# Projection moved into the last attention head of a transformer block with routed experts

## The chip, the cores and the metric

The kernel runs on one core of a Trainium2 chip. The metric is device microseconds of one execution, from a launch to its end. Time before: 2275.77 us, the median of 3 runs (2271.68 to 2276.74).

## What is computed

One block of a vision transformer on 48 x 48 tokens (S = 2304) of width C = 384, batch 1, in float32. Attention has 12 heads of 32 columns with a relative position bias by row and by column; then a projection with bias and the residual; then a layer norm, a router that picks 2 of 8 experts for each token, and the experts (384 to 1536, GELU, back to 384), added to the residual.

```
x  = x + proj(softmax(q*scale @ k.T + bias_h + bias_w) @ v) + proj_b     # q, k, v from layernorm(x)
t  = layernorm(x)
x  = x + sum over the 2 best experts of gate * (gelu(t @ W1 + b1) @ W2 + b2)
```

## The kernel before, in words

Every product of precision is made of three: a value is split into a high part (a type that TensorE takes at full rate) and a low part, the rest; high x high, high x low and low x high are added up in PSUM.

The program is a row of stages, each with its own instruction lists for the five engines, and a stage starts when the one ahead has ended on all of them: `phase_qkv`, `phase_rel` (the bias tables), `phase_attention`, `phase_proj`, `phase_gates`, `phase_experts`.

**Attention** (`phase_attention`, L524) goes through the heads 0 to 11, with two sets of buffers for keys, queries and values, by the head's parity `par`. A head has 54 **units**: 3 query blocks of 768 columns (`QB`), with 18 key tiles each. In unit k TensorE makes the scores of unit k + 3 (four matmuls, `scores`, L753) and the product of unit k's weights with the values (four matmuls, `pv`, L769, accumulated over the 18 tiles of a block in `ps_o`, with a row of ones in the values that gives the sums of the softmax), and, for the softmax, two matmuls for the next head's row maxima (`half`, L747, into the two banks of `ps_m`). ScalarE takes the exponential of a unit twice (L849 and L855: `p_hi` and `p_f`); the low part `p_lo` = `p_f` - `p_hi` is made by VectorE for two units of three and by GpSimd for the third (`low`, L604, run at L608). VectorE takes the maxima (L896). From unit 12 (`SHIFT`) of the last head on there is no next head, so no maxima. At the end of a block, in unit 17, 35 or 53, ScalarE and VectorE copy `ps_o` to `o_t` (L866, L913).

SP's list for a head (`rest`, L665) is written out by hand: the next head's keys and values (`load_kv`), then for each block b a wait for its last scores, the next head's query rows (`load_rest`, L633, four transfers, 2.1 MB), the wait for the block's copies and its `store` (L657: values to `o_d`, sums to `sums_d`), and `load_max` (L648: a row of maxima to memory and back); after the third block `load_hi` (L620) for the head after the next, which is needed at unit 12. GpSimd's `joined` (L716) waits for a store and adds the second half of the values to `o_d` by an accumulating transfer. All of SP's transfers are on one queue.

**Projection** (`phase_proj`, L1033): the sums of all heads come back as 216 columns on 128 partitions, VectorE takes the reciprocal (L1189), it goes out to `rec_d` and comes back as 12 rows; TensorE spreads these rows over 128 partitions (L1124), VectorE scales the heads' values by them (`o_f`, L1168) and makes the low part `o_lo` (L1170), ScalarE the high part (L1162), TensorE multiplies by the weights (nine matmuls for each of 18 tiles, L1136), VectorE adds the residual (L1177) and takes the statistics (L1184) for the layer norm. Meanwhile GpSimd adds the bias to x (L1114) and splits the first expert's six weight pieces (`split_piece`, L1020).

**Gates and experts**: `phase_gates` (L1205) normalises, stores the normalised rows (L1326), computes the router and the lists, and loads four pieces of the second expert; `phase_experts` (L1610) gathers rows by expert (L1660) and runs 43 slots of 128 rows; VectorE splits the pieces of the experts 1 to 7 there.

## Time and profile before

| | us |
|---|---|
| median of 3 runs | 2275.77 |
| the profiled execution | 2276.39 |
| its span, first to last instruction | 2274.7 |
| TensorE busy in it | 2056.3 (90%) |
| VectorE, ScalarE, GpSimd busy | 1435.9, 1483.6, 923.9 |
| last copy of the accumulator in the attention | at 1450.41 |
| first instruction of the gates | at 1529.06 |
| first matmul of the experts | at 1631.07 |

Times in the rows are microseconds from the span's start, and durations follow them; a duration marked ns, or behind "busy us, mean", is in nanoseconds. PE is TensorE, PEld its weight loads, DVE VectorE, ACT ScalarE, POOL GpSimd, SPq SP's queue of transfers. What stands in brackets behind a row is the time for which the engine idled ahead of it, and what ended that.

### The profile page before, as it was taken

The numbers are of one execution on the slowest core, as the hardware profiler recorded it, in microseconds if no ns is written. First come the engines' busy times: TensorE is split into PE (matmuls) and PEld (weight loads), VectorE is DVE, ScalarE is ACT, GpSimd is POOL, SyncE is SP. The second block draws the span as 40 slices with busy tenths as digits, with TensorE's granted clock in tenths as the row PEclk, the third lists the DMA queues.
The fourth block names the chain that finished last, engine by engine and source line by source line (L and its number), as shares of the span: only waits on it lengthen the run. The fifth ranks groups of instructions, "written<-read, shape, count | busy, mean of one in ns | idle before, by whom it ended". The sixth has DMA issues, their size and how long they took to land. (4 is left out here: it accounts for less than half of the span.)

```text
span 2274.7 us, 34244 instructions
## 1 busy us (share of the span) xinstructions
PE 2056.3 (90%) x11132; PEld 1798.3 (79%) x11132; DVE 1435.9 (63%) x2321; ACT 1483.6 (65%) x2533; POOL 923.9 (41%) x621
## 2 busy tenths in 40 slices
PE   6955589999999999999999999674799999999998
PEld 6932278888888888888888888462688888989997
DVE  5665669999999999999999996386333443120000
ACT  3354078888888888888888889412255555555554
POOL 0061323333333333333333334380555665565553
PEclk9955789999999999999999999787699999999999
DMA  6698934565446555564565544322433443211111
GB/s 211 219 252 273 179 82 75 115 109 107 94 87 132 88 112 92 108 126 78 106 113 106 101 78 100 107 110 86 160 80 107 142 123 101 46 40 29 29 29 15
DMA packets 92823, 247.02 MB, mean 109 GB/s; under 512 B 10169, under 2 KB 44441, under 8 KB 88421
## 3 DMA queue, kind: packets, MB, share of 16 engines
q1 hardware_dynamic: 81024, 223.57, 41.2%
q0 software_dynamic: 10672, 20.46, 5.4%
q8 instruction: 101, 1.65, 0.3%
q10 hardware_dynamic: 960, 0.80, 0.1%
q14 instruction: 66, 0.53, 0.1%
HBM read 179.27 MB, written 65.52 MB: 108 GB/s over the span
## 5 line engine op out<-in xcount | busy, mean ns | idle before, releaser
L896 DVE TENSOR_REDUCE mx<-ps_m 128x1 f32<-128x384 f32 x1212 | 642.4, 553 | 100.5 <-PE ps_m L751 95.2
L608 POOL TENSOR_TENSOR p_lo<-p_f,p_hi 128x768 fp32r<-128x768 f32 x216 | 403.1, 1866 | 715.5 <-ACT p_f L855 715.5
L849 ACT ACTIVATE p_hi<-ps_s 128x768 fp32r<-128x768 f32 x648 | 529.1, 817 | 135.5 <-PE ps_s L765 132.1
L855 ACT ACTIVATE p_f<-ps_s 128x768 f32<-128x768 f32 x648 | 525.8, 811 | 13.2 <-POOL p_lo L608 13.2
L751 PE MATMUL ps_m<-key_hi,query_hi 128*128 128x384 f32 x1240 | 419.7, 345 | 43.5 <-DMA query_hi<-rel_hi_d 30.9
L608 DVE TENSOR_TENSOR p_lo<-p_f,p_hi 128x768 fp32r<-128x768 f32 x432 | 427.5, 990 | 39.5 <-ACT p_f L855 38.5
L762 PE MATMUL ps_s<-query_hi,key_hi 128*128 128x384 f32 x1296 | 338.1, 342 | 12.5 <-DMA query_rest<-m_d 10.4
L775 PE MATMUL ps_o<-p_hi,val 128*65 128x384 f32 x1296 | 331.4, 337 | 5.2 <-POOL p_lo L608 5.0
L765 PE MATMUL ps_s<-query_rest,key_rest 121*128 121x384 f32 x1296 | 331.8, 337 | 0.0
L775 PE MATMUL ps_o<-p_lo,val 128*65 128x384 f32 x1296 | 331.2, 337 | 0.0
L751 PEld LDWEIGHTS ps_m<-key_hi,query_hi 128*128 128x128 f32 x1240 | 232.2, 189 | 89.2 <-DMA query_hi<-rel_hi_d 31.2
L1670 POOL TENSOR_TENSOR h_lo<-h_f,h_hi 128x512 fp32r<-128x512 f32 x129 | 185.7, 1440 | 258.4 <-ACT h_hi L1798 256.1
L1782 ACT COPY z_sb<-ps_z 128x512 f32<-128x512 f32 x129 | 75.8, 588 | 265.4 <-PE ps_z L1724 265.4
L762 PEld LDWEIGHTS ps_s<-query_hi,key_hi 128*128 128x128 f32 x1296 | 231.4, 189 | 21.9 <-issue 11.4
L765 PEld LDWEIGHTS ps_s<-query_rest,key_rest 121*128 121x128 f32 x1296 | 238.0, 189 | 0.0
L1724 PE MATMUL ps_z<-w_ring,xg_hi 128*128 x774 | 223.8, 397 | 4.8 <-POOL xg_lo L1666 4.8
L1745 PE MATMUL ps_o<-w_ring,h_hi 128*128 x1032 | 214.7, 350 | 11.6 <-POOL h_lo L1670 11.6
L775 PEld LDWEIGHTS ps_o<-p_lo,val 128*65 128x65 f32 x1296 | 175.2, 135 | 50.6
L775 PEld LDWEIGHTS ps_o<-p_hi,val 128*65 128x65 f32 x1296 | 175.9, 136 | 33.4 <-POOL p_lo L608 8.5
L1745 PEld LDWEIGHTS ps_o<-w_ring,h_hi 128*128 128x128 f32 x1032 | 175.4, 188 | 15.4 <-issue 15.2
L1724 PEld LDWEIGHTS ps_z<-w_ring,xg_hi 128*128 128x128 f32 x774 | 144.6, 189 | 29.0 <-issue 5.2
L1792 ACT ACTIVATE h_f<-ps_h,b_sb 128x128 f32<-128x128 f32 x516 | 147.8, 370 | 6.7 <-issue 1.2
(247 smaller groups left out, 2242.7 us busy)
## 6 DMA issues: line engine op xcount, KB each, us to landing
query_rest<-rel_lo_d SPq DMA_DIRECT2D x36, 864.0 KB
query_rest<-qk_lo_d SPq DMA_DIRECT2D x36, 576.0 KB
query_rest<-qk_hi_d SPq DMA_DIRECT2D x36, 576.0 KB
query_hi<-rel_hi_d SPq DMA_DIRECT2D x12, 864.0 KB, 17.0
w_raw__19867<-w_u SPq DMA_DIRECT2D x12, 768.0 KB, 5.3
w_raw__19868<-w_u SPq DMA_DIRECT2D x12, 768.0 KB, 4.6
w_raw__19869<-w_u SPq DMA_DIRECT2D x12, 768.0 KB, 4.4
w_raw__19870<-w_u SPq DMA_DIRECT2D x12, 768.0 KB, 4.4
```

The lines of the kernel that those rows point to most:

```text
L608: engine.tensor_tensor(p_lo[r][:], p_f[idx % 2], p_hi[r][:].bitcast(F32), ALU.subtract).then_inc(lo_done(0, idx)[0], 1)
L751: pe.matmul(ps[:, c, 0:TB], query_hi[tp][:, tile], key_hi[tp][:, keys], start=True, stop=True).then_inc(mm_ok, 1)
L762: pe.matmul(ps_s[:, bank + c, 0:TB], key_hi[par][:, j * P:(j + 1) * P], query_hi[par][:, b * QB + c * TB:b * QB + (c + 1) * TB], start=Tru ...
L765: last = pe.matmul(ps_s[:, bank + c, 0:TB], key_rest[par][:, j * P:(j + 1) * P], query_rest[b][:, j // 3, c * TB:(c + 1) * TB], start=Fals ...
L775: last = pe.matmul(ps_o[0:VW, c, 0:TB], val[par][:, j, :], part[r][:, c, :], start=(j == 0 and part is p_hi), stop=(j == TILES - 1 and par ...
L849: act.activation(p_hi[r][:], ps_s[:, bank:bank + 2, 0:TB], ACT.Exp).then_inc(hi_ok, 1)
L855: act.activation(p_f[idx % 2], ps_s[:, bank:bank + 2, 0:TB], ACT.Exp).then_inc(f_ok, 1)
L896: dve.tensor_reduce(mx[s // TILES][:, s // 3 % 6, col:col + 1], ps_m[:, c, 0:TB], AX.X, ALU.max).then_inc(mx_ok, 1)
L1670: pool.tensor_tensor(h_lo[u % H_RING][:], h_f[u % 2][:], h_hi[u % H_RING][:].bitcast(F32), ALU.subtract).then_inc(hlo_ok, 1)
L1724: last = pe.matmul(ps_z[:, u % 2, :], v[s % 2][:, k, :], moe.ring[:, cols], start=(n == 0), stop=(n == 8))
L1745: last = pe.matmul(ps_o[:, s % 2, 0:C], v[u % H_RING][:, b, :], moe.ring[:, cols], start=(c == 0 and n == 0), stop=(c == CHUNKS - 1 and n ...
L1792: last = act.activation(h_f[u % 2][:, b, :], ps_h[:, u % 2, b, :], ACT.Gelu, bias=bias)
```

## The change

`phase_proj` is taken out. Heads are numbered from 0; the last is head 11.

- **SP** (`rest`): `store` moves ahead of the wait for the block's scores and of `load_rest`, in every head. In head 10, behind the query loads of its first block, the sums of heads 0 to 7 are loaded (`flat_early`), and their values into `room`; after its second block the reciprocals go out to `rec_d`. After its third block come eight `spread` transfers (each a row of `rec_d` broadcast to 32 partitions of `share`), the sums and values of heads 8 to 10, x, their reciprocals and three more `spread` rows, and `load_max` of the last head's third block behind all of these. The projection's weights are loaded at the end of head 8's list.
- **GpSimd**: `joined` of the last head's blocks goes. In head 10 it makes the high parts of the projection's weights, in the last head the high parts (`high_part`) of the 18 tiles.
- **VectorE**: in head 10 at unit 22 it waits for `flat_early` and takes the reciprocal. In the last head: low parts of the weights (`low_weights`, units 1 and 2); nine products `scale` of `room` by `share` (units 4, 5, 6, 8, 9, 10 and 18, 19, 20), a second reciprocal at unit 12; then, by tile, `low_part` two units ahead of the product and `added` one unit behind it.
- **TensorE** (`tail`): 18 tiles ("all") of nine matmuls over heads 0 to 10 and the bias, in units 26 to 48, and 18 tiles ("own") of three matmuls over head 11 straight from its accumulator copy, with two columns more that give its sums: six in units 29 to 34, six in units 43 to 48, and six after the last unit. They take turns with the two banks of `ps_m`.
- **ScalarE** copies both halves of `ps_o` as high parts in the last head, VectorE subtracts for the low parts; `added` divides an own tile by its sums (a reciprocal of one column, then a multiply-add).
- **Weight pieces**: the first four are loaded at the start of the gates in place of the second expert's first four; GpSimd splits two of them there, and SP waits for each split before it loads the fifth and sixth piece, ahead of the third and fourth store of the normalised rows. VectorE splits the other four at the start of the experts.
- Buffers are placed so that x, `share` and the parity-0 keys and queries can share room.

```diff
+EARLY = 2 * HPT
+LATE = HEADS - 1 - EARLY
+FIRST_TILE = 26
+SPLITS_AT = [11, 14]
+WEIGHTS_AT = [1, 2]
+SCALES_AT = [4, 5, 6, 8, 9, 10, 18, 19, 20]
+SPLIT_EARLY = 2
...
+            steps.setdefault(FIRST_TILE + 4 * t // 3, []).append(("all", t))
+            steps.setdefault((29 + t if t < TPQ else 37 + t) if t < 2 * TPQ else UNITS, []).append(("own", t))
...
+            def load_x(g):
+
+                rows = slice(g * TPQ, (g + 1) * TPQ)
+                sp.wait_ge(scaled, QBLOCKS * (g + 1))
+                sp.dma_start(x1[:, rows, :], x.rearrange("(t p) c -> p t c", p=P)[:, rows, :]).then_inc(x_in[g], 16)
+
+            def joins(n):
+                for g in range(2):
+                    sp.wait_ge(ot_out[g], 16 * ((n + 1 - g) // 2))
+                    sp.wait_ge(low_out[g], 16 * ((n + 1 - g) // 2))
+
+            def spread(c, heads):
+                for h in range(heads):
+                    row = rec_d[c * HPT + h:c * HPT + h + 1, :].broadcast_to([HD, S])
+                    sp.dma_start(share[h * HD:(h + 1) * HD, c, :], row).then_inc(spread_in[c], 16)
+
             def rest(h, par):
                 sp.wait_ge(pv_ok, UNITS * h + RING)
                 load_kv(h + 1, 1 - par)
                 for b in range(QBLOCKS):
 
+                    store(h, par, b)
                     sp.wait_ge(s_ok, UNITS * h + TILES * (b + 1))
                     load_rest(h + 1, b)
-                    store(h, par, b)
+                    if h == HEADS - 2 and b == 0:
+                        joins(QBLOCKS * EARLY)
+                        sp.dma_start(flat_early[:], flat(sums_d, 0, EARLY)).then_inc(sums_in, 16)
+                        for c in range(2):
+                            sp.dma_start(room[:, c, :], o_d[c * P:(c + 1) * P, :]).then_inc(early_in, 16)
+                    if h == HEADS - 2 and b == 1:
+                        sp.wait_ge(rec_ok, 1)
+                        sp.dma_start(flat(rec_d, 0, EARLY), flat_early[:]).then_inc(rec_out, 16)
                     if b < 2:
                         load_max(h + 1, b)
                 if h < HEADS - 2:
                     sp.wait_ge(s_ok, UNITS * (h + 1) + LEAD)
                     load_hi(h + 2, par)
+                else:
+                    sp.wait_ge(s_ok, UNITS * (h + 1))
+                    sp.wait_ge(rec_out, 16)
+                    for c in range(2):
+                        spread(c, HPT)
+                    joins(QBLOCKS * (HEADS - 1))
+                    sp.dma_start(flat_late[:], flat(sums_d, EARLY, LATE)).then_inc(sums_in, 16)
+                    sp.wait_ge(raw_zero, 5)
+                    sp.dma_start(room[0:P - HD, 2, :], o_d[2 * P:C - HD, :]).then_inc(late_in, 16)
+                    load_x(0)
+                    sp.wait_ge(rec_ok, 2)
+                    sp.dma_start(flat(rec_d, EARLY, LATE), flat_late[:]).then_inc(rec_out, 16)
+                    sp.wait_ge(rec_out, 32)
+                    spread(2, LATE)
                 load_max(h + 1, 2)
+                if h == HEADS - 4:
+                    load_weights()
+                if h == HEADS - 2:
+                    load_x(1)
+                    load_x(2)
...
+            def tail(kind, t):
+
+                n = number_of[kind, t]
+                if n == 0:
+                    pe.wait_ge(mx_ok, 2 * UNITS * HEADS)
+                if n >= 2:
+                    pe.wait_ge(evicted, n - 1)
+                if n == 0:
+                    pe.wait_ge(w_low, 2)
+                if kind == "all":
+                    pe.wait_ge(low_ok, t + 1)
+                    hi, lo = part_hi[t % len(part_hi)], lows[:, :, t * P:(t + 1) * P]
+                    for m, (v, w) in enumerate([(hi, w_hi), (hi, w_lo), (lo, w_hi)]):
+                        for k in range(KC):
+                            last = pe.matmul(ps_m[:, n % 2, 0:C], v[:, k, :], w[:, k, :], start=(m + k == 0), stop=(m == 2 and k == KC - 1))
...
+            def scale(n):
+
+                c, cols = n // QBLOCKS, slice(n % QBLOCKS * QB, (n % QBLOCKS + 1) * QB)
+                rows = P if c < 2 else P - HD
+                if n == 0:
+                    dve.wait_ge(early_in, 32)
+                if n == 6:
+                    dve.wait_ge(late_in, 16)
+                if n % QBLOCKS == 0:
+                    dve.wait_ge(spread_in[c], 16 * (HPT if c < 2 else LATE))
+                dve.tensor_tensor(room[0:rows, c, cols], room[0:rows, c, cols], share[0:rows, c, cols], ALU.mult).then_inc(scaled, 1)
...
+                    if h == HEADS - 2 and k == TILES + 4:
+                        dve.wait_ge(sums_in, 16)
+                        dve.reciprocal(flat_early[:], flat_early[:]).then_inc(rec_ok, 1)
+                    if last and k in WEIGHTS_AT:
+                        low_weights(WEIGHTS_AT.index(k))
+                    if last and k in SCALES_AT:
+                        scale(SCALES_AT.index(k))
+                    if last and k == 12:
+                        dve.wait_ge(sums_in, 32)
+                        dve.reciprocal(flat_late[:], flat_late[:]).then_inc(rec_ok, 1)
...
+                    if last:
+                        for job in order:
+                            if unit_of[job] == k + 2 and job[0] == "all":
+                                low_part(job[1])
+                        for job in order:
+                            if unit_of[job] == k - 1:
+                                added(*job)
...
-            for i in range(PIECES, PIECES + RAWS):
+            for i in range(RAWS):
                 moe.load_piece(sp, i)
+            sp.dma_start(moe.b1_sb[:], moe.b1_t).then_inc(moe.b_in, 16)
             for blk in range(BLOCKS):
+                if 2 <= blk < 2 + SPLIT_EARLY:
+                    sp.wait_ge(moe.w_ok, blk - 1)
+                    moe.load_piece(sp, RAWS + blk - 2)
                 sp.wait_ge(xn_ok, blk + 1)
...
+            for part in range(SPLIT_EARLY, PIECES):
+                moe.split_piece(dve, part)
             for e in range(1, EXPERTS):
```

## Rows read from the trace of the kernel before

**Rows 1.** By stage: window, us, busy PE, PEld, DVE, ACT, POOL, clock, DMA, GB/s

```profile
1270.00:1367.00 97.00, 96.04 (x543) 85.35 (x543) 87.94 (x151) 83.40 (x114) 35.71 (x21) 1.00 0.54 102
1398.00:1424.00 26.00, 25.60 (x145) 21.21 (x143) 13.96 (x13) 25.77 (x37) 11.81 (x7) 1.00 0.38 122
1450.40:1529.00 78.60, 51.78 (x198) 40.99 (x198) 48.22 (x51) 8.58 (x8) 53.62 (x22) 0.76 0.39 130
1479.00:1529.00 50.00, 43.40 (x186) 37.35 (x186) 40.27 (x46) 5.80 (x5) 44.97 (x16) 0.88 0.22 83
```

**Rows 2.** Timeline, start and duration in us: the end of the attention and the gates' beginning

```profile
1450.41 0.48 ACT L866 COPY o_t<-ps_o 65x384 f32<-65x384 f32 x1 [2.89 <-PE ps_o L775]
...
1529.06 0.29 SPq L1321 DMA_DIRECT2D b_raw<-b  x1
```

**Rows 3.** Timeline of VectorE in the projection: three additions of the residual

```profile
1509.98 1.47 DVE L1177 TENSOR_TENSOR x<-ps_y,x 128x384 f32<-128x384 f32 x3
```

**Rows 4.** Timeline of TensorE in the projection: two groups of three matmuls

```profile
1490.40 0.68 PE L1136 MATMUL ps_y<-pw_lo,o_hi 128*128 128x384 f32 x3
1490.92 0.68 PE L1136 MATMUL ps_y<-pw_hi,o_lo 128*128 128x384 f32 x3
```

**Rows 5.** Timeline of GpSimd in head 10: the join of the first block

```profile
1320.97 0.78 POOL L721 DMA_DIRECT2D o_d<-o_t  x1 [4.40 <-DMA o_d<-o_t]
```

**Rows 6.** Timeline of ScalarE: the accumulator's copies at units 17, 35, 53 of head 10

```profile
1302.12 0.48 ACT L866 COPY o_t<-ps_o 65x384 f32<-65x384 f32 x1 [0.23 <-PE ps_o L775]
...
1335.10 0.48 ACT L866 COPY o_t<-ps_o 65x384 f32<-65x384 f32 x1 [0.23 <-PE ps_o L775]
...
1367.22 0.48 ACT L866 COPY o_t<-ps_o 65x384 f32<-65x384 f32 x1 [0.23 <-PE ps_o L775]
```

**Rows 7.** Timeline of SP's queue: `load_hi`; stores of head 10; query loads

```profile
1272.38 0.42 SPq L625 DMA_DIRECT2D query_hi<-rel_hi_d  x1
...
1303.04 1.25 SPq L661 DMA_DIRECT2D o_d<-o_t  x1
...
1364.81 0.43 SPq L642 DMA_DIRECT2D query_rest<-qk_lo_d  x1
...
1368.07 0.32 SPq L661 DMA_DIRECT2D o_d<-o_t  x1
```

**Rows 8.** Transfers' size and us to landing: issued at 1272.38, 1303.04, 1368.07

```profile
query_hi<-rel_hi_d SPq DMA_DIRECT2D x1, 864.0 KB, 18.1
...
o_d<-o_t SPq DMA_DIRECT2D x1, 96.0 KB, 17.6
...
o_d<-o_t SPq DMA_DIRECT2D x1, 96.0 KB, 13.2
```

**Rows 9.** Timeline of TensorE: the first maximum of unit 12 of head 10

```profile
1293.04 0.34 PE L751 MATMUL ps_m<-key_hi,query_hi 128*128 128x384 f32 x1
```

**Rows 10.** Timeline of VectorE: units 22 (head 10), 4 (last head); the projection's preparations

```profile
1311.55 0.56 DVE L896 TENSOR_REDUCE mx<-ps_m 128x1 f32<-128x384 f32 x1 [0.31 <-PE ps_m L751]
...
1376.65 0.56 DVE L896 TENSOR_REDUCE mx<-ps_m 128x1 f32<-128x384 f32 x1 [0.34 <-PE ps_m L751]
...
1460.56 1.50 DVE L1189 RECIPROCAL rflat<-rflat 128x216 f32<-128x216 f32 x1 [9.59 <-DMA rflat<-sums_d]
...
1466.70 1.36 DVE L1191 TENSOR_TENSOR pw_lo<-pw_raw,pw_hi 128x1152 fp32r<-128x1152 f32 x1 [4.64 <-ACT pw_hi L1157]
```

**Rows 11.** As rows 1, in the projection: a gap of TensorE and after it

```profile
1516.20:1520.10 3.90, 0.51 (x3) 0.19 (x2) 3.90 (x3) 0.00 (x0) 3.90 (x2) 1.00 0.00 0
...
1521.30:1524.20 2.90, 2.90 (x11) 2.90 (x11) 1.72 (x4) 0.00 (x0) 2.90 (x1) 0.50 0.00 0
```

**Rows 12.** What the transfers moved from 1364 to 1384, in 40 slices

```profile
GB/s 0 0 0 86 98 276 276 221 221 215 221 215 215 203 197 227 258 147 141 152 160 178 154 141 141 141 119 98 68 43 49 37 12 0 0 0 0 43 98 55
```

**Rows 13.** Timeline of GpSimd in the projection: a piece's subtraction

```profile
1503.95 3.49 POOL L1030 TENSOR_TENSOR w_ring<-w_raw__19869,w_ring 128x1536 fp32r<-128x1536 f32 x1
```

**Rows 14.** Groups from 1483.9 to 1501.7: busy us, mean ns | idle before

```profile
L1170 DVE TENSOR_TENSOR o_lo<-o_f,o_hi 128x1152 fp32r<-128x1152 f32 x3 | 10.1, 3354 | 3.7 <-ACT o_hi L1162 3.7
```

365 lines of the change are left out of this document (174 added, 191 removed).

## The prediction

> **What bounds the kernel now.** I read the busy time by stage first, then the seams between stages on the timeline, then SP's queue with its transfers' landings. In the attention TensorE is busy 96.0 of the 97.0 us of a head; VectorE, at 87.9, is close behind it, so work added to VectorE there is not free [rows 1]. From unit 12 of the last head on the maxima are over: VectorE is busy 14.0 of 26 us, while TensorE (25.6) and ScalarE (25.8) share the bound. In the 78.6 us that follow TensorE is busy only 51.8, at a mean clock of 0.76: transfers, reciprocals and VectorE set the pace of the projection, and that is the stretch which the change removes. Gates and experts keep their order but for the weight pieces.
>
> The sum is made against the profiled execution, 2276.39 us (span 2274.7 and 1.7 around it), which is 0.6 above the median of 2275.77. A measurement of this kernel can tell a change of about 0.2%, 4.6 us.
>
> **1. The stage that goes.** ScalarE's last copy of the accumulator starts at 1450.41 and the first instruction of the gates at 1529.06 [rows 2]: 78.65 us. In its place stands what follows the last product with the values: two copies of 0.48 and the subtractions behind them, so that the first own product starts some 1.2 us later, and then six own tiles, which VectorE paces: a multiply-add from PSUM (0.5, a third of the 1.47 of three additions [rows 3]), a statistics call of the same length, a reciprocal of one column, and waits between the three. That is 1.0 us for a tile at least; I take 1.3, so 7.8 for six, and 0.5 for the last statistics, 0.3 for the change of stage, 1 for latencies: 10.8. **-67.8 us** (-70 to -65).
>
> **2. The products move into the last head.** A tile's nine matmuls cost three times 0.52, as groups of three start 0.52 apart at full clock [rows 4]: 1.57. Eighteen of these and twelve own tiles of three matmuls (0.52) are 34.5 us of TensorE, in units 26 to 48. Little of it hides, since TensorE and ScalarE were both full [rows 1]: I take off 1.2 for what slack there was, and add 2.1 for tiles that wait for VectorE. **+35.4** (32 to 43).
>
> **3. The store goes ahead of the next head's loads.** Now GpSimd's `joined` waits for a store that lies behind 2.1 MB of query loads, 4.40 us at 1320.97 [rows 5]; its next p_lo is then late, ScalarE waits for it and TensorE for ScalarE. The block in which that falls takes 32.98 us (copies at 1302.12 and 1335.10), the next 32.12 [rows 6]. Over heads 1 to 10 the ten blocks of this kind take 10.3 us more than 32.06 each. With the store ahead of the loads the wait has no cause. **-10** (-13 to -6).
>
> **4. The price of that order.** In the third block the query loads began 3.3 us ahead of the store (1364.81 and 1368.07 [rows 7]); now they begin 0.6 behind it, 3.9 later. Behind them lies `load_hi`, whose last part is issued at 1272.38 and lands 18.1 later, at 1290.5 [rows 7, 8]; the first maximum that needs it runs at 1293.04 [rows 9]. So 2.5 of slack against 3.9: up to 1.4 late here, by the same reckoning less in most other heads. **+3.5** over ten heads (0 to 12).
>
> **5. A new wait in head 10.** `flat_early` is issued behind the query loads of the first block, and VectorE waits for it at unit 22. What stands behind these loads now, the store issued at 1303.04, lands 17.6 us later, at 1320.6 [rows 7, 8]; unit 22's first maximum runs at 1311.55 [rows 10]. So VectorE stands for 9.1 us and then takes the reciprocal of 144 columns (1.50 x 144/216 = 1.0 [rows 10]). TensorE stops one unit later, as each half of `ps_m` waits for its maximum, and so do p_lo and all behind it: 9.5. After 3.9 us in which it was mostly idle TensorE ran 2.9 us at the lower of its clocks, 1.2 GHz [rows 11], so 1.5 more. **+11** (0 to 13).
>
> **6. The same in the last head.** The query loads of the third block start at about 1368.7, behind the store. Now, what is issued behind them lands 16.5 us after their start (1364.81 to 1368.07 + 13.2 [rows 7, 8]), so they are through at about 1385. Next come the eight `spread` rows; `scale(0)` waits for the first four, 1.15 MB. No row shows this load. The rates of the query loads bound it, 276 GB/s at their best and 141 near their end [rows 12]: 4.2 to 8.2 us. I take 215, their plateau, since both are broadcast into some 32 rows at a time: 5.4, less 1.5 for the falling end of the older loads: 1389 (1386 to 1394). VectorE comes to unit 4 at 1376.65 [rows 10], so TensorE is held 12.4 us, in which `low_weights` hides (1.36 for 1152 columns [rows 10], and 0.5). The six scalings, each two thirds of that in columns, 0.95, add 5.7, less 1.2 of VectorE's slack; with 1.5 for the clock, **+18.4** (6 to 24).
>
> **7. The third chunk.** Its chain (join, sums, reciprocal at unit 12, store, wait, three rows) ends at about 1418.5, and VectorE comes to unit 18 at about 1416.8; two copies in place of one at unit 17 add 0.5. **+2.2** (0 to 8). `load_max` of the third block now stands behind that chain on SP, but it is wanted only at unit 33, some 20 us later, and the loads of x, which wait for the scalings, at unit 26: nothing for both; if the chain were over 20 us late, unit 33 would wait for the rest.
>
> **8. Gates and experts.** Two pieces are split on GpSimd at the start of the gates, where it idled (3.49 us for a subtraction beside VectorE [rows 13]); SP waits for them ahead of the third and fourth store of the normalised rows, and the rows behind them have one block's time to spare: +1 (0 to 4). The other four are split by VectorE as the experts begin, beside GpSimd's gathers; there it splits the second expert's pieces today, which come later now: between nothing and the length of one such subtraction, +1.5. **+2.5** (0 to 7.5).
>
> The sum: -67.8 + 35.4 - 10 + 3.5 + 11 + 18.4 + 2.2 + 2.5 = -4.8, and 2276.4 - 4.8 = 2271.6; I say 2271.5.
>
> **Rival A: the small transfers are not held up behind the query loads**, and both long waits fall away: -11 of step 5 and -12 of step 6 give 2271.5 - 23 = 2248.5; one of the two about 2260. For it: nothing in the program orders `flat_early` or `spread` behind these loads but the queue. Against it: today's stores land 17.6 and 13.2 us after their issue behind them [rows 8]. The Trainium skill (DMA: Bandwidth & Descriptors, section Queues, rings and completion order) says that transfers of one issuing engine need not end in their order, since each is split over up to 16 rings and one on few of them can overtake; 2248.5 is what that would give here, but rows 8 speak for queueing. Chance 0.22.
>
> **Rival B: VectorE paces the tiles in units 26 to 48**, and the change ends slower. In the old projection's steady stretch TensorE was busy 43.4 of 50.0 us for 18 tiles, waiting for VectorE, so 0.37 idle for a tile, at a clock of 0.88 [rows 1]. If the 30 tiles go like that: 30 x 0.37 = 11.1, and 34.5/0.88 - 34.5 = 4.7, less the 2.1 that I have: +13.7, 2285. It decides once a tile waits 0.4 us on the average (12 us, less 2.1, turns -4.8 into over +4.6). For it: the same order of work (a low part ahead of the product, an addition behind it, two banks), with two thirds of the p_lo in the same stream, and `low_part`, like `o_lo`, takes two inputs from SBUF beside GpSimd: 3.35 us for 1152 columns there [rows 14] against 1.36 alone [rows 10]. Against it: each low part is made two units ahead, and VectorE's work, 18 for p_lo (0.78 a unit [rows 1]), 20 for low parts at the contended price, 9 for additions and 15.6 for own tiles, is 63 us against TensorE's 67. The Trainium skill (SBUF — State Buffer, section Who interferes with whom) says that a VectorE instruction with two SBUF inputs contends with a GpSimd one that reads SBUF, and that the later one blocks; rows 14 agree, and the rule speaks against `low_part` in this place. Chance 0.24.
>
> **How the numbers follow.** My own case has 0.54; its own range is 2263 to 2281 (4 either way for `spread`, some 6 for the tiles, the smaller terms). With A and B in part the range that holds 8 in 10 is 2250 to 2287. Faster by over 0.2%, so below 2271.2: all of A (0.22) and nearly half of mine (0.26), 0.48. Within 0.2%: 0.23, all of it mine. Slower: 0.05 of mine and B, 0.29.
>
> **What would show it.** Right: the first gates instruction about 11 us behind the last copy of the accumulator; no wait of `joined`, and all blocks of heads 1 to 9 at about 32.1 us, with waits of TensorE for `query_hi` of at most 1.4; VectorE idle for some 9 us ahead of the reciprocal of `flat_early` and for some 10 ahead of the first scaling; TensorE dense in units 26 to 48. Wrong: no such idle time in heads 10 and 11 (A), or TensorE waiting for VectorE all through those units (B).

## The result and the profile after

The changed kernel takes 2292.92 us (median of 6 runs, 2291.82 to 2297.35), the kernel before 2276.26 (6 runs, 2270.29 to 2280.99): a ratio of 1.0079, 95% interval 1.0067 to 1.0091. It is slower by 0.8%, 6 us above the upper end of the forecast's range (2287) and 21 above the forecast (2271.5). The profiled execution of the changed kernel took 2297.35, 4.4 above its median; its span is 2295.6, 20.9 more than the span before.

The timeline gives the seams: ScalarE's copies of the accumulator from head 10 on (in the last head they are the high parts `ot_hi`), and the gates' first instruction.

```profile
1270.34 0.48 ACT L1027 COPY o_t<-ps_o 65x384 f32<-65x384 f32 x1 [0.21 <-PE ps_o L896]
1303.71 0.47 ACT L1027 COPY o_t<-ps_o 65x384 f32<-65x384 f32 x1 [0.23 <-PE ps_o L896]
...
1432.73 0.85 ACT L1022 CAST ot_hi<-ps_o 65x384 fp32r<-65x384 f32 x2 [0.15 <-PE ps_o L896]
1479.76 0.85 ACT L1022 CAST ot_hi<-ps_o 65x384 fp32r<-65x384 f32 x2 [2.60 <-PE ps_o L896]
1531.11 0.85 ACT L1022 CAST ot_hi<-ps_o 65x384 fp32r<-65x384 f32 x2 [2.88 <-PE ps_o L896]
...
1542.08 0.30 SPq L1383 DMA_DIRECT2D b_raw<-b  x1
```

The two copies between them start at 1348.63 and 1380.82. Differences of such starts, in the traces of both kernels, account for the 20.9 us:

| stretch | before | after | difference | forecast |
|---|---|---|---|---|
| start to the first copy | 329.30 | 325.55 | -3.75 | 0 |
| units 18 to 35, heads 0 to 9 | 331.55 | 321.77 | -9.78 | -10 (step 3, with head 10) |
| the ten blocks that hold unit 12 of heads 1 to 10 | 320.65 | 334.79 | +14.14 | +3.5 (step 4) |
| units 36 to 53, heads 0 to 10 | 352.74 | 353.79 | +1.05 | 0 |
| units 18 to 35, head 10 | 32.98 | 44.92 | +11.94 | +11 (step 5) |
| last head, first block | 30.71 | 51.91 | +21.20 | +18.4 (step 6) |
| last head, second and third block | 52.48 | 98.38 | +45.90 | +37.6 (steps 2, 7) |
| last copy to the gates | 78.65 | 10.97 | -67.68 | -67.8 (step 1) |
| gates, to the experts' first product | 102.01 | 106.51 | +4.50 | +2.5 (step 8) |
| experts | 643.63 | 647.01 | +3.38 | with the gates |

The first line is not shown to be an effect of the change: the kernels below that have the changed kernel's code there reach the first copy between 323.9 and 328.6, and the one that has the old code at 328.39.

**The waits.** TensorE's timeline shows where it stood; the bracket is the idle time ahead and its releaser. First come two of the ten waits at unit 12 (the longest, and head 10's), then units 22 of head 10 and 4 of the last head, then two in the tiles.

```profile
512.74 0.44 PE L872 MATMUL ps_m<-key_hi,query_hi 128*128 128x384 f32 x1 [2.34 <-DMA query_hi<-rel_hi_d]
...
1294.51 0.44 PE L872 MATMUL ps_m<-key_hi,query_hi 128*128 128x384 f32 x1 [0.91 <-DMA query_hi<-rel_hi_d]
...
1324.69 0.69 PE L872 MATMUL ps_m<-key_hi,query_hi 128*128 128x384 f32 x1 [9.99 <-DVE mx L1057]
...
1406.82 0.69 PE L872 MATMUL ps_m<-key_hi,query_hi 128*128 128x384 f32 x1 [13.65 <-DVE mx L1057]
...
1440.38 0.90 PE L896 MATMUL ps_o<-p_hi,val 128*65 128x384 f32 x2 [2.97 <-POOL p_lo L657]
...
1482.74 0.78 PE L914 MATMUL ps_m<-pw_hi,part_hi 128*128 128x384 f32 x3 [2.30 <-DVE x L1094]
```

The two long ones name VectorE, which was itself waiting. VectorE's timeline names the transfers:

```profile
1323.17 1.05 DVE L1126 RECIPROCAL flat_early<-flat_early 128x144 f32<-128x144 f32 x1 [10.35 <-DMA flat_early<-sums_d]
...
1405.34 0.96 DVE L1080 TENSOR_TENSOR room<-room,share 128x768 f32<-128x768 f32 x1 [14.02 <-DMA share<-rec_d]
```

Both were issued behind 2.1 MB of query loads. The list of transfers has their landings: `load_hi` of head 10 (issued at 1274.47), the sums, the spread rows, and the store, which now goes ahead of the query loads (before: 17.6 and 13.2 [rows 8]).

```profile
query_hi<-rel_hi_d SPq DMA_DIRECT2D x1, 864.0 KB, 20.0
...
flat_early<-sums_d SPq DMA_DIRECT2D x1, 72.0 KB, 16.0
...
share<-rec_d SPq DMA_DIRECT2D x8, 288.0 KB, 18.0
...
o_d<-o_t SPq DMA_DIRECT2D x1, 96.0 KB, 1.8
```

By stretch (us, busy PE, PEld, DVE, ACT, POOL, clock, DMA, GB/s): the block of head 10's long wait, and the last head's three.

```profile
1303.70:1348.60 44.90, 34.71 (x182) 30.62 (x181) 30.06 (x52) 27.88 (x38) 12.48 (x7) 0.89 0.54 127
1380.80:1432.70 51.90, 35.45 (x172) 27.74 (x172) 34.62 (x50) 27.82 (x38) 14.65 (x7) 0.87 0.69 151
1432.70:1479.80 47.10, 43.24 (x227) 38.49 (x227) 30.79 (x46) 27.49 (x39) 24.23 (x17) 0.93 0.16 51
1479.80:1531.10 51.30, 46.90 (x253) 42.42 (x251) 31.11 (x55) 24.60 (x34) 17.14 (x13) 0.97 0.00 1
```

Before, the last two blocks held 50.5 us of TensorE's work in 52.5 (25.9 and 24.56 by the same view); now they hold 90.1 in 98.4. So 39.7 of the 45.9 us is TensorE's time, 34.5 of products and, by difference, some 5 for the lower clock (0.93 and 0.97, where it was 1.00 before), and 6.2 is idle time.

**The gates.** VectorE's timeline before, then VectorE's and GpSimd's after:

```profile
1532.86 3.17 DVE L1492 TENSOR_SCALAR xnn<-x,mv,rstd 128x384 f32<-128x384 f32 x6
1535.94 0.17 DVE L1505 TENSOR_TENSOR g_lo<-g_raw,g_hi 128x24 fp32r<-128x24 f32 x1
```

```profile
1545.92 8.77 DVE L1561 TENSOR_SCALAR xnn<-x,mv,rstd 128x384 f32<-128x384 f32 x6
...
1554.60 3.42 DVE L1574 TENSOR_TENSOR g_lo<-g_raw,g_hi 128x24 fp32r<-128x24 f32 x1
...
1549.51 3.42 POOL L1264 TENSOR_TENSOR w_ring<-w_raw__20454,w_ring 128x1536 fp32r<-128x1536 f32 x1
...
1554.55 3.43 POOL L1264 TENSOR_TENSOR w_ring<-w_raw__20455,w_ring 128x1536 fp32r<-128x1536 f32 x1
```

A subtraction of 24 columns took 0.17 us and now takes 3.42, and it starts 0.05 behind GpSimd's subtraction of 3.43: VectorE stood until GpSimd was through. The Trainium skill (SBUF — State Buffer, section Who interferes with whom) has this as a lock on a shared port pair that the later one waits for; the trace agrees.

### The profile page after: what moved, and what is told of

It is laid out like the page before. It is cut to its first block and busy times, and to the rows that moved or that the text cites. A ratio compares the mean times of both kernels' runs of the same rounds, so it can differ in the third digit from the quotient of the medians.

```text
span 2295.6 us, 34382 instructions
## 1 busy us (share of the span) xinstructions
PE 2062.2 (90%) x11150; PEld 1810.0 (79%) x11150; DVE 1452.4 (63%) x2385; ACT 1477.7 (64%) x2529; POOL 905.7 (39%) x626
## 5 line engine op out<-in xcount | busy, mean ns | idle before, releaser
L657 DVE TENSOR_TENSOR p_lo<-p_f,p_hi 128x768 fp32r<-128x768 f32 x432 | 413.2, 957 | 42.0 <-ACT p_f L1006 42.0
L883 PE MATMUL ps_s<-query_hi,key_hi 128*128 128x384 f32 x1296 | 337.2, 341 | 10.4 <-DMA query_rest<-m_d 8.8
L886 PE MATMUL ps_s<-query_rest,key_rest 121*128 121x384 f32 x1296 | 336.4, 341 | 0.0
L883 PEld LDWEIGHTS ps_s<-query_hi,key_hi 128*128 128x128 f32 x1296 | 235.1, 190 | 17.6 <-issue 9.6
```

Source lines behind the costliest of these rows:

```text
L657: engine.tensor_tensor(p_lo[r][:], p_f[idx % 2], p_hi[r][:].bitcast(F32), ALU.subtract).then_inc(lo_done(0, idx)[0], 1)
L883: pe.matmul(ps_s[:, bank + c, 0:TB], key_hi[par][:, j * P:(j + 1) * P], query_hi[par][:, b * QB + c * TB:b * QB + (c + 1) * TB], start=Tru ...
L886: last = pe.matmul(ps_s[:, bank + c, 0:TB], key_rest[par][:, j * P:(j + 1) * P], query_rest[b][:, j // 3, c * TB:(c + 1) * TB], start=Fals ...
```

## The experiments

One table first: medians, then lengths from the same starts as above (ten blocks with unit 12; block 18 to 35 of head 10; the three blocks of the last head), and the gates' start to the router's first reduction.

| kernel | us | ten blocks | head 10 | last head | gates |
|---|---|---|---|---|---|
| before | 2276.26 | 320.65 | 32.98 | 30.71, 26.27, 26.21 | 36.00 |
| changed | 2292.92 | 334.79 | 44.92 | 51.91, 47.03, 51.35 | 40.01 |
| 1 `load_hi` first | 2279.96 | 321.22 | 45.61 | 50.78, 45.74, 49.84 | 38.46 |
| 2 sums first | 2282.58 | 334.39 | 32.50 | 51.09, 45.83, 51.18 | 39.72 |
| 3 spread rows first | 2281.19 | 333.99 | 44.58 | 38.92, 43.51, 49.83 | 40.07 |
| 4 no split on GpSimd | 2290.88 | 333.59 | 44.70 | 52.43, 46.11, 51.40 | 36.66 |
| 5 SP's waits late | 2293.40 | 337.14 | 44.13 | 52.77, 46.00, 51.36 | 39.78 |
| 6 edits 1 to 4 | 2252.17 | 321.24 | 32.50 | 37.89, 45.83, 49.83 | 36.16 |
| 7 and late scalings | 2248.67 | 321.25 | 32.50 | 35.80, 46.07, 47.23 | 36.60 |
| 8 as 7, early join | 2252.37 | 321.37 | 32.51 | 36.34, 46.70, 47.25 | 36.68 |
| 9 as 8, high parts on ScalarE | 2277.01 | 321.43 | 32.51 | 37.87, 61.51, 60.57 | 36.74 |
| 10 as 7, query loads last | 2245.85 | 321.21 | 32.51 | 32.42, 46.04, 47.26 | 36.68 |
| 11 as 10, a third of the products | 2234.22 | 321.30 | 32.50 | 32.46, 44.80, 39.90 | 35.68 |
| before, with SP's order of 1 | 2261.59 | 320.57 | 32.10 | 30.68, 26.24, 26.20 | |

The theory throughout: the change's losses are separate waits for transfers that stand behind query loads on SP's queue, and VectorE and GpSimd in each other's way.

**1. `load_hi` ahead of the third block's query loads.**

```diff
+                    if h < HEADS - 2 and b == 2:
+                        load_hi(h + 2, par)
                     load_rest(h + 1, b)
...
-                if h < HEADS - 2:
-                    sp.wait_ge(s_ok, UNITS * (h + 1) + LEAD)
-                    load_hi(h + 2, par)
-                else:
+                if h == HEADS - 2:
```

> The changed kernel with one edit: in the third block of heads 0 to 9 load_hi is issued ahead of load_rest. Theory (the price of the new order): in the changed kernel the third part of load_hi lands 23.6 to 25.5 us behind the block's copy, where the first maximum of unit 12 wants it at 23.0; the ten blocks that hold unit 12 take 33.5 us on the average in place of 32.05. With load_hi ahead of 2.1 MB of query loads it lands some 8 us earlier, so these ten blocks go back to 32.0 to 32.2 each and the kernel takes about 14 us less (12 to 15): about 2279, within 0.2% of the kernel before or a little above. Rival (the blocks are longer because stores, joins and loads now collide on the transfer engines, not because of the order on SP's queue): the ten blocks keep most of their excess, under 5 us less. What it could cost: load_rest of the third block lands about 7 us later, and is wanted only 33 units on.

Measured: 13.0 us less than the changed kernel (ratio to before 1.0016, interval 1.0004 to 1.0029); the ten blocks take 321.22, 32.1 each, and no wait for `query_hi` is left. It was the order on the queue.

**2. The sums ahead of head 10's first store.**

```diff
                 load_kv(h + 1, 1 - par)
+                if h == HEADS - 2:
+                    joins(QBLOCKS * EARLY)
+                    sp.dma_start(flat_early[:], flat(sums_d, 0, EARLY)).then_inc(sums_in, 16)
                 for b in range(QBLOCKS):
...
                     if h == HEADS - 2 and b == 0:
-                        joins(QBLOCKS * EARLY)
-                        sp.dma_start(flat_early[:], flat(sums_d, 0, EARLY)).then_inc(sums_in, 16)
```

> The changed kernel with one edit: the load of flat_early, with the joins ahead of it, is issued ahead of head 10's first store, not behind the query loads of its first block. Theory (it is held up behind 2.1 MB of query loads): VectorE's 10.35 us of idle time ahead of the first reciprocal and TensorE's 9.99 go away, the block of units 18 to 35 of head 10 takes 32.1 plus about 1 for the reciprocal in place of 44.9, and the kernel takes 11 to 13 us less, about 2281. Rival (the load of sums as 128 rows is slow by itself, or the two loads of values beside it hold it up): the wait shrinks by under 4 us. A second rival: the time is given back at the first scaling of the last head, whose wait for the spread rows grows by as much; then the kernel takes under 3 us less. By the theory that wait stays at 14.0, since the spread rows are issued by units, not by time.

Measured: 10.3 less (1.0031, 1.0019 to 1.0043). The same 72 KB land 6.4 us after their issue in place of 16.0, the reciprocal at unit 22 has no wait, and the block takes 32.50. The wait in the last head did not grow (13.21 for 14.02).

```profile
1313.19 1.04 DVE L1127 RECIPROCAL flat_early<-flat_early 128x144 f32<-128x144 f32 x1
```

```profile
flat_early<-sums_d SPq DMA_DIRECT2D x1, 72.0 KB, 6.4
```

**3. The spread rows ahead of the last query loads.**

```diff
                     sp.wait_ge(s_ok, UNITS * h + TILES * (b + 1))
+                    if h == HEADS - 2 and b == 2:
+                        sp.wait_ge(rec_out, 16)
+                        for c in range(2):
+                            spread(c, HPT)
                     load_rest(h + 1, b)
...
-                    sp.wait_ge(s_ok, UNITS * (h + 1))
-                    sp.wait_ge(rec_out, 16)
-                    for c in range(2):
-                        spread(c, HPT)
```

> The changed kernel with one edit: the eight spread rows are issued ahead of the query loads of head 10's third block. Theory (they are held up behind those loads): they start at about the copy of the accumulator and need 1.15 MB for the first four, 4.2 to 8.2 us at 276 to 141 GB/s, so they are in at about 6 to 10 us behind the copy, and VectorE comes to the first scaling 9.6 us behind it: of its 14.0 us of idle time 0 to 2 is left. The block takes about 36 to 38 us in place of 51.9, the kernel 13 to 16 us less, about 2278. Rival (the broadcast rows are slow in themselves, as each of 256 descriptors reads the same 9 KB row): the wait keeps over 6 us and the kernel takes under 8 us less. A new wait is possible at the second reciprocal (unit 12), whose chain starts from GpSimd's join at unit 8 and which the long stall covers today: up to 5 us.

Measured: 11.7 less (1.0021, 1.0009 to 1.0032), a little under what was expected. The eight rows land 6.8 us after their issue (median) in place of 18.0, the first scaling has no wait, and the block takes 38.92. Of the 8.2 us that are left above 30.71, six scalings of 0.95 in units that are full of maxima would make 5.7; that is an estimate. At unit 18 the first scaling of the third chunk now waits 2.1.

```profile
1392.40 1.03 DVE L1080 TENSOR_TENSOR room<-room,share 128x768 f32<-128x768 f32 x1
```

```profile
share<-rec_d SPq DMA_DIRECT2D x8, 288.0 KB, 6.8
```

**4 and 5. The pieces in the gates: no split on GpSimd, or the splits kept and SP's waits moved.**

```diff
-SPLIT_EARLY = 2
+SPLIT_EARLY = 0
```

```diff
-                if 2 <= blk < 2 + SPLIT_EARLY:
-                    sp.wait_ge(moe.w_ok, blk - 1)
-                    moe.load_piece(sp, RAWS + blk - 2)
...
+            for i in range(SPLIT_EARLY):
+                sp.wait_ge(moe.w_ok, i + 1)
+                moe.load_piece(sp, RAWS + i)
             sp.wait_ge(moe.b_in, 16)
```

> The changed kernel with one edit: GpSimd splits no weight piece in the gates, VectorE splits all six as the experts begin. Theory (VectorE is blocked beside GpSimd's subtractions): in the changed kernel the first group of VectorE's normalisations takes 8.77 us where it took 3.17, and a subtraction of 24 columns takes 3.42, as long as GpSimd's subtraction beside it, where it took 0.17. Without the splits the gates up to the first gather take 4.0 us less, as before; the experts' start has two more pieces for VectorE, 5.4 us, of which the later pieces are wanted only by the second product, so 0 to 2 us come back: in all 2 to 4 us less than the changed kernel. Rival (SP's two waits for the splits hold up the stores of the normalised rows): the same time goes, but in the trace the normalisations stay at 8.8 us with no GpSimd work beside them, which this run would show at once. The next run with the splits kept and the waits moved tells the two apart by time.

> The changed kernel with one edit: GpSimd still splits two pieces in the gates, but SP waits for the splits, and loads the fifth and sixth piece, only behind the last store of the normalised rows. Theory (VectorE is blocked by GpSimd's subtractions): nothing changes in the gates; the normalisations' first group still takes 8.8 us, the router's first reduction still comes 40.0 us after the gates' start, and the kernel takes what the changed kernel takes, 2291 to 2294. Rival (the prediction's own cause, SP's waits for the splits ahead of the stores): the reduction comes 36 to 37 us after the gates' start and the kernel takes 3 to 4 us less.

Measured: 2.0 less without the splits (1.0063, 1.0046 to 1.0079, which overlaps the changed kernel's interval), no change with the waits moved (2293.40; 1.0080, 1.0064 to 1.0096). The times alone do not tell the two apart. VectorE's lines do; first without the splits, then with them and with SP's waits moved:

```profile
1543.07 3.10 DVE L1561 TENSOR_SCALAR xnn<-x,mv,rstd 128x384 f32<-128x384 f32 x6
1546.10 0.17 DVE L1574 TENSOR_TENSOR g_lo<-g_raw,g_hi 128x24 fp32r<-128x24 f32 x1
```

```profile
1544.99 8.76 DVE L1561 TENSOR_SCALAR xnn<-x,mv,rstd 128x384 f32<-128x384 f32 x6
...
1553.68 3.41 DVE L1574 TENSOR_TENSOR g_lo<-g_raw,g_hi 128x24 fp32r<-128x24 f32 x1
```

The prediction's cause, SP's waits, is out; GpSimd's subtractions are the cause, 3.4 us in the gates. From the gates' start to the reduction the kernels with the splits take 38.5 to 40.1 us, those without 35.7 to 36.7.

**6. The four edits together** (those of runs 1, 2, 3 and 4).

> The changed kernel with the four edits of the first four runs together (load_hi first, sums first, spread rows first, no split on GpSimd). These took 13, 10, 12 and 2 us off the changed kernel one by one. Theory (four separate waits on the path, each with its own cause): they add up, 37 us less than the changed kernel, 2254 to 2258, so the change is then some 0.9% faster than the kernel before. Rival (they are one stall that moves: with one wait gone, the next transfer on SP's queue or the chain of the third chunk stops VectorE): a new wait of 5 us or more at unit 12 or 18 of the last head, and 2262 to 2275.

Measured: 2252.17, 40.8 less than the changed kernel (the four alone: 13.0 + 10.3 + 11.7 + 2.0 = 37.0); 0.9897 of before, 0.9879 to 0.9914. They add up: these are separate waits. A wait of 3.5 us at the first scaling of the third chunk is there, less than the 5 that the rival asked for.

**7. The scalings behind the maxima.**

```diff
-SCALES_AT = [4, 5, 6, 8, 9, 10, 18, 19, 20]
+SCALES_AT = [13, 14, 15, 16, 18, 19, 21, 22, 23]
```

```diff
-                        dve.wait_ge(pv_ok, UNITS * h + k + 1 + RING)
                         if last:
+                            for job in order:
+                                if unit_of[job] == k - 1:
+                                    added(*job)
+                            dve.wait_ge(pv_ok, UNITS * h + k + 1 + RING)
                             for c in range(2):
                                 dve.wait_ge(acc_a, ACC + 2 * b + c + 1)
...
                         for job in order:
-                            if unit_of[job] == k - 1:
+                            if unit_of[job] == k - 1 and k % TILES < TILES - 1:
                                 added(*job)
```

```diff
-                    load_x(0)
                     sp.wait_ge(rec_ok, 2)
...
                 if h == HEADS - 2:
+                    load_x(0)
                     load_x(1)
```

> The kernel with the four edits, and three more in the last head: the scalings go to units 13 to 16, 18, 19 and 21 to 23, where no maxima are taken; x is loaded behind the last spread rows; and at unit 35 VectorE takes the addition that is due ahead of the subtractions for the accumulator. With the spread rows first, the last head's first block still took 38.9 us where it took 30.7 before; of the 8.2 us, 5.7 are the six scalings in units where VectorE had no slack and the rest GpSimd's p_lo beside them (2.6 and 3.0 us for 1.8). Theory (VectorE is the bound in units 0 to 12 and not behind them): the block goes to 32 to 34 us, the second to under 45 and the third keeps 48 to 50, as the wait of 2.3 us at unit 35 goes too; 5 to 9 us less than the kernel with four edits, 2246 to 2251. Rival (two-input work on VectorE beside GpSimd costs the same wherever it stands): the blocks together take what they took, within 2 us.

Measured: 3.5 less (2248.67; 0.9878, 0.9859 to 0.9896), under the 5 to 9 that were expected (2246 to 2251 held, as run 6 had come out lower), and each block missed what was said of it. The third went from 49.83 to 47.23, below the 48 to 50, with the wait of 2.3 gone. The second stayed at 46.07 and not under 45. The first only went from 37.89 to 35.80, not to 32 to 34: a wait for the sums of heads 8 to 10 had appeared (first line), and at the start of the second block one of GpSimd's `p_lo` took 5.14 us for 1.8. The rival is out all the same: the three blocks together take 4.5 less.

```profile
1385.60 0.49 DVE L1137 RECIPROCAL flat_late<-flat_late 128x54 f32<-128x54 f32 x1 [4.00 <-DMA flat_late<-sums_d]
...
1394.67 5.14 POOL L657 TENSOR_TENSOR p_lo<-p_f,p_hi 128x768 fp32r<-128x768 f32 x1 [3.48 <-ACT p_f L1006]
```

**8. GpSimd's join at unit 5, not 8**, for the last block of head 10.

```diff
-                    if idx % TILES == JOIN and idx < UNITS and 0 <= n < QBLOCKS * (HEADS - 1):
+                    if idx % TILES == JOIN and idx < UNITS and 0 <= n < QBLOCKS * (HEADS - 1) - 1:
                         joined(n)
+                    if h == HEADS - 2 and idx == UNITS + 5:
+                        joined(QBLOCKS * (HEADS - 1) - 1)
```

> The kernel with seven edits (2248.7 us), and GpSimd's join of head 10's third block at unit 5 of the last head in place of unit 8. With the long stall gone, the chain of the third chunk (join, sums of heads 8 to 10, reciprocal at unit 12) is late: VectorE idles 4.00 us for the sums there, and TensorE 2.5 for the p_lo behind it. Theory (the chain starts from the join): three units earlier are 5.3 us, so the wait is gone and the last head's first block takes 31.5 to 33 us in place of 35.8; 3 to 5 us less, 2244 to 2246. Rival (the store ahead of the join, or the load of sums behind the third block's query loads, sets the landing): the wait keeps over 2 us and the time changes by under 2.

Measured: 2252.37 (0.9898, 0.9882 to 0.9913), no gain; the wait is 4.52, as the rival said. In run 7 the sums were issued as soon as the join's transfer had landed, and landed 1.7 us later; that transfer itself took 11.6 us, where it takes 2.7 once the query loads stand behind the chain (run 10). In run 8 the join came 5.2 us earlier, counted from the accumulator's last copy in head 10, and its transfer took 8.6; the sums were issued 8.2 earlier (at 1377.20) and now took 10.4. So an earlier join is of no use: the query loads hold up whichever of the two transfers falls beside them, and the join's is on GpSimd's own queue, not on SP's.

```profile
1387.65 0.49 DVE L1139 RECIPROCAL flat_late<-flat_late 128x54 f32<-128x54 f32 x1 [4.52 <-DMA flat_late<-sums_d]
```

```profile
flat_late<-sums_d SPq DMA_DIRECT2D x1, 27.0 KB, 10.4
```

The join's transfer in run 7, then in run 10:

```profile
o_d<-o_t POOLq DMA_DIRECT2D x1, 96.0 KB, 11.6
...
o_d<-o_t POOLq DMA_DIRECT2D x1, 96.0 KB, 2.7
```

**9. The tiles' high parts on ScalarE** (`high_part` taken out of GpSimd's list, with its waits).

```diff
                         exps(h + (up != par), up, idx, turned_at(k, last))
+                    if last:
+                        for t in range(TILES):
+                            if unit_of["all", t] - 2 == k:
+                                high_part(t)
```

> As the run with the early join, and the 18 high parts of the tiles are made by ScalarE, not by GpSimd. In the last two blocks of the last head TensorE's added work is 34.5 us, and both together took 40.8 us more than before in the run with the late scalings. Theory (VectorE's two-input low parts and scalings and GpSimd's reads hold each other up there): GpSimd's p_lo go from 2.1 back to 1.8 us and VectorE's low parts from 0.85 to 0.55, and the two blocks take 1 to 3 us less. Rival (TensorE is the bound in these blocks but for a few waits, and ScalarE has the copies on its path): no change within 1 us, or up to 3 us more, as a copy of about 0.5 us on ScalarE then stands ahead of an exponential in 18 of 24 units, in which ScalarE has 1.6 of work for a unit of some 3.

Measured: 2277.01 (0.9999, 0.9989 to 1.0009), 24.6 more than run 8; a miss on both sides. The list of waits (us in total, times, longest) shows where the time went: VectorE waited 39.1 us for high parts, which in ScalarE's list stand behind exponentials (three of their four buffers lie in the room of `val` and carry its name), and TensorE 16.9 for VectorE's additions to the large tiles, which stand behind the low parts.

```profile
DVE lows L1087 <- ACT val L990: 27.6, 12, 6.8
DVE lows L1087 <- ACT part_hi L990: 11.5, 3, 6.1
```

So it tells nothing of the contention that it was to measure.

**10. The last head's third query loads behind the third chunk.**

```diff
-                    load_rest(h + 1, b)
+                    if not (h == HEADS - 2 and b == 2):
+                        load_rest(h + 1, b)
...
                     spread(2, LATE)
+                    load_x(0)
+                    load_rest(h + 1, 2)
...
                 if h == HEADS - 2:
-                    load_x(0)
                     load_x(1)
```

> The kernel with seven edits (2248.7 us), and the query loads of the last head's third block (2.1 MB, wanted at unit 33) are issued behind the chain of the third chunk, not ahead of it. The run with the early join left VectorE's wait for the sums at 4.5 us: there the load of sums was issued at about 1377 and landed at 1387. Theory (that load too is held up behind the query loads): without them the sums are in ahead of unit 12, the wait of 4.0 us is gone, and the spread rows of the third chunk come as early; the last head's first block takes 31 to 33 us in place of 35.8, and the kernel 3 to 5 us less, 2244 to 2246. Rival (GpSimd's join is late by itself): the wait keeps over 2 us. What it could cost: the query loads now share the engines with x, and unit 33 waits if they land more than some 20 us late.

Measured: 2245.85 (0.9867, 0.9852 to 0.9883), 2.8 less than run 7, and the lowest of the versions that make all the products: 47 less than the changed kernel, 1.3% less than before. The reciprocal has no wait, and the block takes 32.42, 3.4 less than in run 7; this tells the two apart, as the intervals overlap.

```profile
1381.08 0.48 DVE L1139 RECIPROCAL flat_late<-flat_late 128x54 f32<-128x54 f32 x1
```

**11. What paces the tiles**: the 18 large tiles with three matmuls in place of nine.

```diff
-                    for m, (v, w) in enumerate([(hi, w_hi), (hi, w_lo), (lo, w_hi)]):
-                        for k in range(KC):
-                            last = pe.matmul(ps_m[:, n % 2, 0:C], v[:, k, :], w[:, k, :], start=(m + k == 0), stop=(m == 2 and k == KC - 1))
+                    for k in range(KC):
+                        last = pe.matmul(ps_m[:, n % 2, 0:C], hi[:, k, :], w_hi[:, k, :], start=(k == 0), stop=(k == KC - 1))
```

> As the run with the query loads behind the chain, but each of the 18 tiles over heads 0 to 10 makes only the first three of its nine matmuls, so that the products with the low parts are left out there; everything else, VectorE's low parts too, is done. It asks what paces units 26 to 48. Theory of the forecast (TensorE is the bound there, with single waits at the seams): 108 matmuls less at 0.174 us are 18.8 us, and 15 to 19 go. Rival (VectorE paces the tiles): TensorE's time goes into waits for the additions, and under 6 us go.

Measured: 11.6 less than run 10 (2234.22; 0.9812, 0.9799 to 0.9825), between the two. It splits by block: the second lost 1.2 us of its 46.0, the third 7.4 of 47.3; the profiled executions differ by 10.8, and the 2.2 that are left lie in stretches that the edit does not touch. Eight of the 18 tiles lie at units 26 to 35, 8.4 us of the left-out work; ten at 36 to 48, 10.4. By stretch the second block of run 10, then the second and third of run 11:

```profile
1388.40:1434.40 46.00, 42.13 (x227) 37.44 (x226) 38.62 (x54) 27.77 (x38) 26.38 (x17) 0.96 0.54 126
...
1387.00:1432.00 45.00, 36.53 (x186) 30.18 (x185) 40.53 (x55) 28.09 (x39) 25.98 (x17) 0.96 0.54 129
1432.10:1472.00 39.90, 34.55 (x187) 29.12 (x186) 31.59 (x51) 24.64 (x34) 18.38 (x13) 1.00 0.00 1
```

In run 11 VectorE is the fuller in the second block, 40.5 of 45.0 against TensorE's 36.5, and TensorE waits 4.9 us for its additions (0.6 in run 10); in the third TensorE is the fuller. With all the products TensorE is the fuller in the second block too (42.1 against 38.6). So with five of the scalings in it that block stays at some 45 us even with 8.4 us less for TensorE to do: VectorE's bound lies 1.2 under what the block takes. TensorE bounds the third. In the changed kernel three scalings stand there; that was not tried.

**12. SP's order alone, on the kernel before.**

```diff
+                    store(h, par, b)
                     sp.wait_ge(s_ok, UNITS * h + TILES * (b + 1))
+                    if h < HEADS - 2 and b == 2:
+                        load_hi(h + 2, par)
                     load_rest(h + 1, b)
-                    store(h, par, b)
...
-                if h < HEADS - 2:
-                    sp.wait_ge(s_ok, UNITS * (h + 1) + LEAD)
-                    load_hi(h + 2, par)
```

> The kernel before, with only SP's order changed: the store ahead of the query loads, and load_hi ahead of the third block's query loads. Theory (the join's wait and the late load_hi are two ends of the same queue): the ten blocks of units 18 to 35 go from 32.2 to 33.9 to 32.1 to 32.2, which is 10 us less in all, the ten blocks that hold unit 12 stay at 32.0 to 32.2, and the kernel takes 9 to 11 us less than before, about 2266, with no other part of the change. Rival (the gain of the order needs the rest of the change, or is given back in another block): under 4 us less.

Measured: 2261.59 (0.9937, 0.9923 to 0.9952), 14.1 less than before, above the 9 to 11 that were expected. The profiled execution is 3.7 above this median, and its span is 11.1 less than before; the eleven blocks of units 18 to 35, at 32.0 to 32.1 each, make 11.7 of that. So of the 30.4 us by which run 10 beats the kernel before, more than a third (11.1 in the traces, 14.1 by the medians) needs no part of the projection's move.

## Why the prediction was wrong

Most of the mechanisms held: the waits of steps 4, 5 and 6 came at their places and for the transfers that the prediction names. Step 7's wait did not come, and step 8 had another cause. The sum failed, by 25.7 in the profile (-4.8 forecast, +20.9 measured), of which 4.4 is the distance of the profiled execution from its median. Three terms make nearly all of the 25.7: step 4 with 10.6, steps 2 and 7 with 8.3, step 8 with 5.4. The -3.75 of the table's first line, which no step has, worked the other way by luck.

- **Step 1** held: 10.97 for 10.8. The six last tiles came 1.1 to 1.26 apart, where 1.3 was taken.
- **Step 3** held: -9.8 in heads 0 to 9, and some 0.8 more within head 10's block. There are eleven such blocks, not ten: head 0 has one too.
- **Step 4 is the step that failed**: "+3.5 over ten heads (0 to 12)", measured +14.1 and, by run 1, 13.0 in the median. Its cause held, since run 1 removes it by the order alone; its size did not. For head 10 the reckoning was close: 1.4 late forecast, 1.1 measured, and the block grew by 1.27. What was wrong is "less in most other heads", for which the prediction shows no reckoning: all ten are late. Measured behind the block's copy, the landing came at 18.8 to 21.5 us before (mean 19.7) and comes at 23.6 to 25.5 now (mean 24.3), where unit 12 wants it at 23.0. So the mean slack was 3.3, better than the 2.5 of head 10, but the mean delay was 4.5 and not 3.9: the last part of `load_hi` is issued 2.0 later and takes 2.5 longer to land. TensorE's waits at unit 12 sum to 10.95, the longest 2.34, where the prediction gave 1.4 as the most; the other 0.3 a block is not placed.
- **Steps 2 and 7** were too low by 8.3: +45.9 for 37.6. The 34.5 us of products is right. The waits and the lower clock were put at 3.1 with the third chunk's, and came to 11.4: 6.2 idle and some 5 of clock. Two of the waits are in no step: GpSimd's `p_lo` behind three scalings of the third chunk (2.97 us), and at unit 35 VectorE's subtraction of the accumulator standing ahead of an addition that TensorE waits for (2.30; gone in run 7). The wait that step 7 does have, VectorE's at unit 18 for the third chunk, did not come: the first scaling there, at 1435.11, waited for nothing. It came once the long wait at unit 4 was gone, with 2.1 us in run 3 and 3.5 in run 6.
- **Step 8** was too low by 5.4, and for another cause. 4.5 is the gates, where the prediction counted SP's waits and took GpSimd's splits as free because GpSimd idled; they block VectorE, for 3.4 of the 4.5 (run 4). The other 3.4 is the experts' stage, and about two thirds of that came without the change too, in run 12 (last section).
- **Steps 5 and 6** held but for size: +12.8 (against a block of 32.1) for 11, and +21.2 for 18.4. TensorE stood 9.99 where 9.5 was worked out, and 13.65 where 12.4 was; VectorE idled 10.35 for 9.1, and 14.02 for some 10.
- **Rival A**, that small transfers would not queue, is out. The Trainium skill (DMA: Bandwidth & Descriptors, section Queues, rings and completion order) allows a transfer on few rings to overtake. Here none did: the sums, the spread rows and the late sums landed 16.0, 18.0 and 10.4 us after their issue behind the query loads, and 6.4, 6.8 and 1.7 ahead of them or after their end. On how many rings each of them ran, no trace here shows.
- **Rival B**, that VectorE paces the tiles, was half right. Most tiles were dense (the longest single waits make 5.3 of the 8.3 us of idle time), but run 11 shows that, with five scalings in it, VectorE's own bound on the second block lies only 1.2 us under TensorE's. The prediction weighed VectorE's work against TensorE's over both blocks together (63 us and 67), and not block by block.

With its waits taken out (run 10) the kernel is 30.4 us faster than before, 14.1 of which SP's order brings alone (run 12): so the projection's move is worth some 16 us by the medians, 20 by the spans of the two profiled executions, once VectorE no longer waits for its transfers.

## What to carry to other kernels

When a transfer is moved ahead on a queue, work out the slack of everything that now stands behind it in every round of the loop, not in one. Here every small transfer issued behind megabytes on the same queue landed 9 to 16 us later than ahead of them, and one on another queue was held up too (11.6 us for 2.7), so issue what an engine in the critical loop waits for ahead of what is wanted a block later. An idle engine is not a free one: look at what its operands share with the engine beside it.

## What was not expected of the hardware

GpSimd can be held for longer than one instruction of VectorE. In the changed kernel its `p_lo` at 1435.06 took 5.26 us, where the median is 1.84:

```profile
1435.06 5.26 POOL L657 TENSOR_TENSOR p_lo<-p_f,p_hi 128x768 fp32r<-128x768 f32 x1 [3.34 <-ACT p_f L1006]
...
1434.24 0.94 DVE L657 TENSOR_TENSOR p_lo<-p_f,p_hi 128x768 fp32r<-128x768 f32 x1
1435.11 1.82 DVE L1080 TENSOR_TENSOR room<-room,share 96x768 f32<-96x768 f32 x2
1436.85 0.95 DVE L657 TENSOR_TENSOR p_lo<-p_f,p_hi 128x768 fp32r<-128x768 f32 x1
1437.71 0.95 DVE L1080 TENSOR_TENSOR room<-room,share 96x768 f32<-96x768 f32 x1
```

VectorE ran five instructions with two inputs from SBUF without a gap, the first of them begun before GpSimd's, until 1438.66; GpSimd ended 1.66 behind that, about its own time. So by the timing it got in only when VectorE's run was over. The same pattern, with 5.14 us, stands in runs 7 and 10.

The experts' stage began at a granted clock that differed between kernels. In its first 16 us it was 0.82 in the kernel before, 0.71 in the changed kernel, 0.88 in run 1 and 0.71 in run 12, as these rows show in that order (columns as in the table by stretch above):

```profile
1631.07:1647.07 16.00, 13.12 (x53) 11.02 (x54) 10.09 (x7) 7.15 (x16) 4.94 (x3) 0.82 0.68 239
...
1648.59:1664.59 16.00, 12.22 (x44) 10.01 (x45) 15.83 (x11) 7.22 (x16) 6.10 (x3) 0.71 0.83 286
...
1630.73:1646.73 16.00, 13.14 (x56) 10.80 (x57) 15.83 (x11) 7.13 (x16) 5.53 (x3) 0.88 0.77 260
...
1617.75:1633.75 16.00, 13.12 (x47) 10.91 (x48) 10.09 (x7) 7.23 (x16) 4.22 (x3) 0.71 0.71 244
```

To the end the stage took 643.6 us before, 647.0 in the changed kernel, 642.9 in run 1, which has the changed kernel's instructions there, and 646.9 to 648.0 in runs 2 to 11. Run 12 has the old kernel's instructions there and took 645.8: at the lower clock the old stage is 2.2 us longer too. So about 2.2 of the 3.4 us is not shown to be a cost of the change. At the same 0.71 the changed stage is 1.2 us longer than the old one (up to 2.2 in the other runs); VectorE's splits, by which it is busy 15.8 of the first 16 us where it was 10.1, could be the cause, but that was not tried. What decides the clock was not found.
